# A two-layer graph network with gathers: the order of work of four engines in conv 2 rearranged

## The reference

```python
def gcn_conv(x, W, b, src, dst):            # conv 1, 2 and 3
    xw = x @ W
    s, d = concat(src, arange(N)), concat(dst, arange(N))    # own row added
    norm = rsqrt(deg)[s] * rsqrt(deg)[d]
    return segment_sum(norm[:, None] * xw[s], d) + b

h = relu(layernorm(x))
g = gelu(layernorm(conv1(h)) * gamma1 + beta1)
x = x + gelu(layernorm(conv2(g)) * gamma2 + beta2 + h)       # x2 in the kernel
x = x + conv3(relu(layernorm(x)))
```

## Time and profile before

| | |
|---|---|
| median of 3 runs | 3725.81 us |
| profiled execution, its time and its span | 3727.32 us, 3725.5 us |
| PE busy | 2958.6 us (79%), 15721 instructions |
| VectorE busy | 2601.0 us (70%), 6384 |
| GpSimd busy | 2131.0 us (57%), 1619 |
| ScalarE busy | 1912.1 us (51%), 2847 |
| bytes moved | 867.71 MB, mean 233 GB/s |
| granted TensorE clock, mean | 0.928 |

### The profile page before, as it was taken

One profiled execution on the slowest core, in us unless ns is written; L12 is line 12 of the kernel. 1 busy time (PEld: TensorE's weight loads), 2 busy tenths in 40 slices (PEclk: granted clock), 3 DMA queues, 4 the chain that ended last, 5 costly groups with the idle time before them and its releaser, 6 DMA issues. The chain is left out here.

```text
span 3725.5 us, 59156 instructions
## 1 busy us (share of the span) xinstructions
PE 2958.6 (79%) x15721; PEld 2469.3 (66%) x15721; DVE 2601.0 (70%) x6384; ACT 1912.1 (51%) x2847; POOL 2131.0 (57%) x1619
## 2 busy tenths in 40 slices
PE   8133399999999967777667667667665999999999
PEld 2022288888888856556556556556554888888888
DVE  9899688888888856776676676676674444454444
ACT  0366477777777645555555555555554333333333
POOL 0122377777777656666666666666664555555553
PEclk9999999999999988888888888888887999999999
DMA  3599888888888657776776676776665999999997
GB/s 114 198 411 418 307 210 215 220 216 212 216 217 215 184 167 207 204 218 201 207 218 197 202 222 199 205 215 202 200 205 185 286 286 290 288 287 286 288 289 211
DMA packets 321119, 867.71 MB, mean 233 GB/s; under 512 B 78801, under 2 KB 79987, under 8 KB 321064
## 3 DMA queue, kind: packets, MB, share of 16 engines
q1 hardware_dynamic: 190120, 682.00, 50.3%
q0 software_dynamic: 130944, 185.08, 27.6%
HBM read 653.10 MB, written 307.81 MB: 258 GB/s over the span
## 5 line engine op out<-in xcount | busy, mean ns | idle before, releaser
L828 POOL DMA_INDIRECT gathered<-H,idx x1062 | 1547.2, 1457 | 607.3 <-DVE idx L1002 304.1
L895 ACT ACTIVATE ahi<-agg 128x1024 fp32r<-128x1024 f32 x354 | 363.4, 1027 | 1300.6 <-PE agg L1184 1113.9
L1177 PE MATMUL agg<-ident,gathered 128*128 128x128 f32 x2832 | 421.8, 298 | 502.0 <-DMA gathered<-H,idx 501.9
L1203 PE MATMUL out<-Whi,ahi 128*128 128x512 f32 x2832 | 792.1, 402 | 0.0
L1203 PE MATMUL out<-Wlo,ahi 128*128 128x512 f32 x2832 | 766.6, 393 | 0.0
L1203 PE MATMUL out<-Whi,alo 128*128 128x512 f32 x2832 | 760.3, 390 | 0.1
L1177 PEld LDWEIGHTS agg<-ident,gathered 128*128 128x128 f32 x2832 | 366.8, 154 | 568.1 <-DMA gathered<-H,idx 530.2
L1008 DVE TENSOR_TENSOR vlo<-gathered,vhi 128x512 fp32r<-128x512 f32 x354 | 244.4, 690 | 638.4 <-ACT vhi L889 445.4
L1203 PEld LDWEIGHTS out<-Wlo,ahi 128*128 128x128 f32 x2832 | 539.5, 191 | 120.7
L1203 PEld LDWEIGHTS out<-Whi,alo 128*128 128x128 f32 x2832 | 531.5, 188 | 112.9 <-DVE alo L1016 0.5
L1203 PEld LDWEIGHTS out<-Whi,ahi 128*128 128x128 f32 x2832 | 528.8, 196 | 92.6
(11 more groups left out here) (168 smaller groups left out, 3262.3 us busy)
## 6 DMA issues: line engine op xcount, KB each, us to landing
gathered<-H SPq DMA_DIRECT2D x351, 512.0 KB
H<-ho SPq DMA_DIRECT2D x250, 512.0 KB, 9.5
x<-in_x_dram SPq DMA_DIRECT2D x165, 512.0 KB, 8.7
X<-x SPq DMA_DIRECT2D x117, 512.0 KB
x<-X SPq DMA_DIRECT2D x117, 512.0 KB
out_dram<-conv SPq DMA_DIRECT2D x117, 512.0 KB
H<-x SPq DMA_DIRECT2D x48, 512.0 KB, 9.6
gathered<-H,idx POOLq DMA_INDIRECT x1062
```

The costliest lines, as they stand in the source:

```text
L828: pool.indirect_dma_start(rows, None, H[q][0:N, :], bass.IndirectOffsetOnAxis(ap=idx[p.slot(4)][:, c:c + 1], axis=0), bounds_check=N - 1, ...
L895: nc.scalar.activation(Ahi[p.slot(2)][:, :], Agg[p.slot(2)][:, :], ACT.Copy)\
L1177: nc.tensor.matmul(agg[:, (2 * f + j) * P:(2 * f + j + 1) * P], own[:, j, fs], ident[:, :], is_transpose=True, start=(f % 2 == 0 and j == ...
L1203: m = nc.tensor.matmul(o, a[u][:, c:c + P], w[q][:, f, :], start=(n == 0 and second), stop=(not second and n == 3 * KD - 1), skip_group_ch ...
```

## The change

```diff
@@ -809,10 +809,10 @@
                             load_root(known, p.after(3), 3)
                         if has(known, 2):
                             load_x(known, p.after(2), 2)
+                        if has(known, -1):
+                            store_x(known, p.after(-1), -1)
                         if has(known, -lag):
                             store_h(known, p.after(-lag), -lag)
-                        if has(known, -1):
-                            store_x(known, p.after(-1), -1)
                     turn(sp, body)
 
                     for stored in ([] if third else [ho_out]) + ([] if first else [xo_out]):
@@ -871,10 +871,10 @@
                                     gather_first(p.after(k))
                         if second and has(known, 0):
                             residual(known, p)
+                        if has(known, 4):
+                            gather_over(known, p.after(4), 4)
                         if second and (has(known, 0) or has(known, -2)):
                             power(p)
-                        if has(known, 4):
-                            gather_over(known, p.after(4), 4)
                         if has(known, 3):
                             gather_first(p.after(3))
                         if first and has(known, 0):
@@ -967,20 +967,22 @@
                             if second:
                                 high(p.after(1))
                                 over_high(p.after(2))
-                                relu_x(0, p)
+                                for k in range(2):
+                                    relu_x(k, p.after(k))
+                                over_high(p.after(3))
                         if second:
-                            if has(known, -2):
-                                squares(p.after(-2))
-                            if has(known, 1):
-                                relu_x(of(known, 1), p.after(1))
+                            if has(known, -1):
+                                squares(p.after(-1))
                             if has(known, 2):
                                 high(p.after(2))
-                            if has(known, 3):
-                                over_high(p.after(3))
+                            if has(known, 0):
+                                gelu(p)
                             if has(known, -2):
                                 relu_x2(of(known, -2), p.after(-2))
-                            if has(known, 0):
-                                gelu(p)
+                            if has(known, 2):
+                                relu_x(of(known, 2), p.after(2))
+                            if has(known, 4):
+                                over_high(p.after(4))
                             return
                         if has(known, 1):
                             high(p.after(1))
@@ -1150,6 +1152,9 @@
                             centre(p)
                         if first:
                             return
+                        if has(known, -1):
+                            x2_sum(of(known, -1), p.after(-1))
+                            x2_mean(p.after(-1))
                         if has(known, -2):
                             x2_scale(p.after(-2))
                         if has(known, 0):
@@ -1158,9 +1163,6 @@
                             x2_shift(p.after(-2))
                         if has(known, 0):
                             normal(known, p, 1)
-                        if has(known, -1):
-                            x2_sum(of(known, -1), p.after(-1))
-                            x2_mean(p.after(-1))
                     turn(dve, body)
 
                 @block.tensor
@@ -1186,29 +1188,40 @@
                                                      start=False, stop=(part is Vlo), skip_group_check=True)
                         m.then_inc(agg_done.sem, 1)
 
-                    def multiply(p, j, known):
-
-                        o, u = Out[2 * p.slot(2) + j][:, :], p.slot(2)
+                    def product(p, j, a, w, stop=False):
+
+                        for f in range(KD):
+                            c = (2 * f + j) * P
+                            m = nc.tensor.matmul(Out[2 * p.slot(2) + j][:, :], a[p.slot(2)][:, c:c + P], w[q][:, f, :],
+                                                 start=False, stop=stop and f == KD - 1,
+                                                 skip_group_check=True)
+                        return m
+
+                    def multiply(p):
+
                         pe.wait_ge(hi_done.sem, hi_done.upto(p))
-                        if not second:
+                        for j in range(2):
                             pe.wait_ge(seeded.sem, seeded.upto(p, j + 1))
-                        elif known is None or known >= 2:
-                            pe.wait_ge(cg_done.sem, cg_done.upto(p.after(-2), j + 1))
-                        n = 0
-                        for a, w in ((Ahi, Whi), (Ahi, Wlo), (Alo, Whi)):
-                            if a is Alo:
-                                pe.wait_ge(lo_done.sem, lo_done.upto(p))
-                            for f in range(KD):
-                                c = (2 * f + j) * P
-                                m = nc.tensor.matmul(o, a[u][:, c:c + P], w[q][:, f, :],
-                                                     start=(n == 0 and second),
-                                                     stop=(not second and n == 3 * KD - 1),
-                                                     skip_group_check=not second)
-                                n += 1
-                        if second:
-                            pe.wait_ge(root_in.of(p), root_in.upto(p))
-                            m = nc.tensor.matmul(o, root[p.slot(4)][:, j, :], B3[:, :], start=False, stop=True)
-                        m.then_inc(main_done.sem, 1)
+                            product(p, j, Ahi, Whi)
+                            product(p, j, Ahi, Wlo)
+                            pe.wait_ge(lo_done.sem, lo_done.upto(p))
+                            product(p, j, Alo, Whi, stop=True).then_inc(main_done.sem, 1)
+
+                    def multiply_second(p, known):
+
+                        pe.wait_ge(root_in.of(p), root_in.upto(p))
+                        for j in range(2):
+                            if known is None or known >= 2:
+                                pe.wait_ge(cg_done.sem, cg_done.upto(p.after(-2), j + 1))
+                            nc.tensor.matmul(Out[2 * p.slot(2) + j][:, :], root[p.slot(4)][:, j, :], B3[:, :],
+                                             start=True, stop=False, skip_group_check=True)
+                        pe.wait_ge(hi_done.sem, hi_done.upto(p))
+                        for j in range(2):
+                            product(p, j, Ahi, Whi)
+                            product(p, j, Ahi, Wlo)
+                        pe.wait_ge(lo_done.sem, lo_done.upto(p))
+                        for j in range(2):
+                            product(p, j, Alo, Whi, stop=True).then_inc(main_done.sem, 1)
 
                     def body(p, known):
                         if known == 0:
@@ -1216,8 +1229,7 @@
                         if has(known, 1):
                             aggregate(p.after(1))
                         if has(known, 0):
-                            for j in range(2):
-                                multiply(p, j, known)
+                            multiply_second(p, known) if second else multiply(p)
                     turn(pe, body)
 
             for flag in (idx_made, sv_made, vhi_done, vlo_done, agg_done, hi_done, lo_done, main_done):
```

## The result

The changed kernel takes **3403.32 us** (median of 4 runs, 3399.35 to 3406.79) against 3725.43 for the kernel before in the same sessions: ratio 0.9139, 95% interval 0.912 to 0.9157. That is 322 us less. The forecast was 142 less and a range that ended at 3500: the sign was right, the size less than half of the truth.

What follows compares the result with a forecast made beforehand. A loop of waits through GpSimd's gathers and TensorE's body was taken to bound conv 2, 25.30 us per two pairs. 56 cycles x (1.40 + 1.08), plus 3 for the tail, made 142 us less: 3584 us, range 3500 to 3665.

Steps and rivals of the forecast that it cites:

- Bound now: In conv 2 a loop of waits through GpSimd's gathers and TensorE's body binds, 25.30 us per two pairs.
- GpSimd's move, 1.40 us per cycle: In conv 2 gather_over(p+4) goes ahead of power(p), so its issue of 1.40 us leaves the loop once per two pairs.
- landing could go either way: SyncE's store_h and loads shift against the gather in conv 2; landing about 2 us less to 0.4 more, taken at 0.
- ScalarE's order, taken at 0: ScalarE's reordered body in conv 2: same work, 6.8 us per pair, new waits covered by idle time, cost 0.
- VectorE's sums, taken at 0: x2_sum and x2_mean move ahead of x2_scale; VectorE's work stays 8.65 us per pair, effect 0.
- Body of TensorE, 1.08 us per cycle less: Clock term in conv 2: the slow body of 10.12 us shortens to the middle between 10.12 and 7.97.
- rival 2: In conv 2 the clock stays up, waits split into some 2 and 4 us, every body 7.97: 3524 us; chance 0.18.
- The cap of 10.6 us per pair: A chain over three pairs in conv 2, 10.6 to 11.3 us per pair, caps what more could be won.
- rival 3: ScalarE's new order becomes the bound in conv 2; slower, 67 us higher, 3793 us; chance 0.07.
- Rivals 1, 3 and 4: Conv 2: 1, alternation stays, 3645 us (0.24); 3, ScalarE's order binds, 3793 (0.07); 4, gain given back, 3726 (0.04).
- TensorE and SyncE, taken at 0: TensorE's new product order and SyncE's store_x ahead of store_h: same products and bytes, each taken at 0.
- waits for gathered rows 40% shorter in sum: A sign to look for: TensorE's waits for gathered rows in conv 2 fall 40% in sum.

Runs made afterwards that it cites:

- pool_only: The kernel before with GpSimd's move alone, the left-over gather ahead of power: 3561.67 us, ratio 0.9559.
- no_pool: The changed kernel with power ahead of the left-over gather again: 3479.65 us, ratio 0.9358.
- act_only: The kernel before with ScalarE's new body (and its first one) and nothing else: 3481.06 us, ratio 0.9351.
- no_dve: The changed kernel with VectorE's x2_sum and x2_mean back behind normal(p, 1), at the end of its body: 3473.38 us, ratio 0.933.
- ahead: The changed kernel with TensorE's old product order, gather_first for p+4 instead of p+3, own rows loaded for p+5 between the two stores: 3353.29 us, ratio 0.9002.
- both_back: The changed kernel with store_h ahead of store_x and TensorE's old product order again: 3388.08 us, ratio 0.9096.

## Why the prediction was right or wrong

- **Bound now**: right. A loop over two pairs through power, gathers, landing and a body of TensorE; its sum matches the period before and after.
- **GpSimd's move, 1.40 us per cycle**: right as a term (pool_only: 2.97, of which 1.40 issue), and no_pool shows that it is still worth 76 us in the changed kernel.
- **The step that failed**: "landing could go either way", bounds 2 us less and 0.4 more, "I take 0, since gather and burst overlap before and after". It fell by 3.51 us, more than the other terms together, 197 of the 321 us. The bounds were the extremes of one pattern, in which store_h came 1.2 us behind the first gather, and ScalarE's order sets that distance. The kernel before did show another one, at the start of conv 2, where the stores have not begun:

```profile
1361.13 1.56 POOL L828 DMA_INDIRECT gathered<-H,idx  x1 [0.30 <-issue]
...
1355.55 0.34 SPq L778 DMA_DIRECT2D x<-in_x_dram  x1
1369.67 0.34 SPq L785 DMA_DIRECT2D X<-x  x1
```

SyncE issues nothing between these two transfers, and the rows issued by 1362.69 are transposed at 1365.64: a landing of 2.95 us. The prediction read that row for the clock only. Two bodies later the gathers are issued by 1382.74, store_h follows at 1383.59, 4.3 us behind the first of them, and the transposes start at 1386.40 without a wait, a landing of 3.7 us at most. So the rows of the kernel before allow a landing over 4 us shorter, and not 2.
- **ScalarE's order, taken at 0**: wrong. It moves relu_x2 and with it store_h; act_only shows 245 us. The prediction followed who waits for ScalarE, and not what its step relu_x2 releases on SyncE's queue, though it named the phase.
- **VectorE's sums, taken at 0**: wrong. With squares(p-1) there is a loop over one pair (mean, squares, high, low, statistics, sums), which was not written down. It decides when the sums stand last: 70 us (no_dve). In the changed kernel it does not bind (2.4 us of waits).
- **Body of TensorE, 1.08 us per cycle less**: right in kind, small in size: 1.84. The waits split, as rival 2 said, because both became short. The sentence that a long wait starts a slow body holds: the granted clock is 0.84 before, 0.96 after, and 1.00 in `ahead`, where no wait for rows is left and those for `sv` end within 1.7 us. The Trainium skill's page TensorE: Matmul & The Clock Gate (section on oscillation) ties the slow starts to waits for DMA, and these three agree.
- **The cap of 10.6 us per pair** by the chain over three pairs had the landing of 8.1 in it. With the landing of 3.84 and the issue, power and body of the table it is some 28.4 us or 9.5 per pair, below the 9.79 measured. A cap that contains the disputed term caps nothing.
- **Issue and power**, not forecast: 0.57 and 0.39 us more per cycle. They are of the kind of rival 3, a new order with a price of its own, but small. Rivals 1, 3 and 4 did not happen: relu_x waits 3.6 us in 900 for x.
- **TensorE and SyncE, taken at 0**: some 15 us against the change together (both_back).
- **A slip in the signs**: "waits for gathered rows 40% shorter in sum" does not follow from the prediction's own numbers, 25.30 - 10.12 - 7.97 = 7.2 us per cycle before and 5.8 forecast, 20% less. Measured are 2.9 us per cycle in the changed kernel.

## What to carry to other kernels

Before a DMA's landing is carried over into a new order, look which other transfers are issued around it, and ask of each moved step what its semaphore releases on the DMA queues: the distance between a burst and a gather is a quantity of its own, and was worth 197 of 321 us here. A loop that goes through an engine twice (sums, squares, high, low) is found by writing down for each step of the new order which step of the same body must precede it on another engine. What was left of the wait behind the latency went away by issuing one step further ahead (42 us).

## What the runs showed that was not expected

The issue of the two gathers took 3.65 to 3.75 us in nine of the kernels and 4.14 to 4.24 where both GpSimd's move and the early sums are in; many of these gathers have some 2.07 us where they had 1.60. In the changed kernel the gather at 2000.47 runs beside the two sums of x2, which VectorE starts at 2000.38:

```profile
2000.38 0.68 DVE L1076 SCALAR_TENSOR_TENSOR x<-x,y 128x512 f32<-128x512 f32 x1
```

and in no_dve, where they come later:

```profile
2001.51 1.60 POOL L828 DMA_INDIRECT gathered<-H,idx  x1 [0.19 <-issue]
```

no_pool tells that it goes with the sums and not with one gather. There the left-over gather stands behind power, and starts while the first sum runs:

```profile
1604.54 0.68 DVE L1076 SCALAR_TENSOR_TENSOR x<-x,y 128x512 f32<-128x512 f32 x1
1604.61 1.57 POOL L828 DMA_INDIRECT gathered<-H,idx  x1 [0.19 <-issue]
```

From 1500 to 2400 us this gather takes 1.57 us in the mean, against 1.07 in the changed kernel, where it stands ahead of power. The first of the two others takes 2.01 us in the changed kernel, beside the sums, and 1.60 in no_dve, without them. So some 0.5 us are the price of the early sums on whichever gather stands there. Why a few beside them escape it (in the changed kernel some take 1.60) stays open.
